# The tail of a decoder kernel's first step in two halves with a bank each, one VectorE division and one ScalarE copy moved forward near the end

## The chip, the cores and the metric

The kernel runs on one core of a Trainium2 chip. The metric is the device time of one execution in microseconds (us), taken as the median of several runs; smaller is better. One execution was also recorded by the hardware profiler, and all rows below come from that one. Times in rows are counted from the start of its span.

## What is computed

The reference is one decoder layer over 16 sequences of 128 tokens and 256 channels: a retention block, a cross-attention block and a feed-forward block, each behind a layer norm and added to its input. Cut to what matters:

```python
x = x + retention(layernorm(x))       # 8 heads of 32
x = x + attention(layernorm(x), ctx)  # 16 heads of 16, causal
x = x + ffn(layernorm(x))             # 8 experts, 256 -> 1024 -> 256, gelu

# retention, the part that the first edit touches
ret   = (ret - mean) * rsqrt(var + 1e-5)      # per token and head of 32
ret   = ret.reshape(B, S, 256) * gn_w + gn_b
gated = x @ W1
out   = (gated * sigmoid(gated) + ret) @ W2
# attention, the part that the second and third edit touch
attn = softmax(where(causal, -inf, q @ k.T * scale))
out  = (attn @ v) @ Wo + bo
```

Expert e serves sequences 2e and 2e + 1, so the kernel's unit of work, two sequences, needs one expert's weights.

## The kernel before, in words

The work is cut into 8 steps of 256 tokens (two sequences, `NB = 2`, of `P = 128` tokens). The three blocks form a software pipeline: iteration `i` of `body` works on the retention of step `a = i`, the attention of step `b = i - 1` and the feed-forward of step `c = i - 2`. Iterations 0, 1, 2 and 7, 8, 9 are written out (with the flags `do_a`, `do_b`, `do_c` and `nextA` saying which blocks take part), 3 to 6 are a hardware loop. Every engine has its own `body`; the order of instructions on an engine is the order of the code, written by hand, and the engines meet through counting semaphores (`signal`, `wait_ge`, `then_inc`). There is no scheduler. Only iteration 0 has a single block in it, so its engines have little else to do while a result goes from one to the next.

**Iteration 0, tail.** The retention output of both sequences lies in PSUM bank `a1` (two halves of 256 columns, one a sequence). GpSimd makes the 16 values of `rstA` (8 heads by 2 sequences) from `varA` with a power of minus one half (`rsqrt`, L454). VectorE multiplies the bank by them into `rnA`, which shares memory with `retT` and is called so in the rows (L1132). TensorE transposes the four 128x128 blocks into bank `a0` (L1671), VectorE scales them with `gn_sb` and adds the gate `silA` to give `outT` (L1151), TensorE multiplies by `W2_sb` into bank `a1` (`to_tokens`, semaphore `s_yA`), VectorE adds `x_keep` to give `x1` (L1161), takes the layer-norm statistics (`statB`, `mvB`), GpSimd makes `rsB`, VectorE normalises into `xnB` (L864), and TensorE transposes `xnB` at the start of iteration 1 (`query_input`, L1246). `projection_low(4, ...)` (the low part of Wo, `xWo_lo`) and the copy of the feed-forward bias (`b1T`) stand on VectorE between the multiplication and the gating. `keep_awake(n)` is `n` matmuls of zeros into a bank that nobody reads: they keep TensorE's activity up while it waits.

**Iteration 7** (`do_b and not nextA`). The softmax sums and the weighted values of a sequence arrive in bank `c0` by `values_to_tokens(seq)` on TensorE (L1422). `divide(seq)` on VectorE is a reciprocal of 16 columns (`rden`, L935) and a multiplication (`att`, L937). `values_to_tokens(1)` writes the same bank, so TensorE waits for `divide(0)` (`s_att`) before it. Behind `values_to_tokens(1)` TensorE has `keys(b0)` and `queries(a, a0)` of step 7, then the score matmuls of iteration 8. ScalarE takes the keys out of PSUM (`kB`, L625), then the queries (`qB`, L638).

**Iteration 8** (`not do_a`). ScalarE's row is: two of four roundings of the second feed-forward weight (`round_w2(2)`, `round_w2(3)`, in the rows `w_hi`), four exponentials (`exps(4)`), the copy of the transposed probabilities (`probT_even(2)`), `exps(5)`, and `ffn_input(b3)` (`xTC_hi`). The third and fourth pair of weight roundings are followed by GpSimd's subtraction (`w2_low`). TensorE's `prob_transposes(3)` needs the copy, because both use bank `b1k`.

## Time and profile before

| | |
|---|---|
| median of 3 runs | 350.05 us |
| the three runs | 350.05, 348.89, 350.06 us |
| the profiled execution | 348.83 us |
| its span, first to last instruction | 347.0 us |
| busy: TensorE, VectorE, ScalarE, GpSimd | 94%, 73%, 69%, 46% |
| granted TensorE clock, mean | 1.000 |

The profiled execution is near the fastest of the three runs, and 1.2 us below their median; 1.8 us of it lie outside the span. A busy share is a mean over the whole span: iterations 0, 1, 8 and 9 are less full than the loop, and there the engines wait for one another.

### The profile page before, as it was taken

To read this page: it belongs to the slowest core of one execution; us is meant where nothing else is said; L and a number is where in the kernel's file an instruction comes from. 1 tells how busy PE (TensorE), PEld (TensorE's weight loads), DVE (VectorE), ACT (ScalarE), POOL (GpSimd) and SP (SyncE) were. 2 spreads that over 40 slices of the span, in tenths; PEclk is the share of its full clock that TensorE was granted. 3 is DMA by queue.
4 is the path that set the end of the run, shared out by engine and by line. 5 is a ranking of instruction groups with operands and counts; after the bars stand their busy time and mean duration, and the time that the engine had idled before them with its cause. 6 is when DMAs were issued, how large, how long until landed. Compare 5 with 4: busy or idle time off the path is not lost.

```text
span 347.0 us, 9380 instructions
## 1 busy us (share of the span) xinstructions
PE 327.2 (94%) x3475; PEld 275.4 (79%) x3475; DVE 254.3 (73%) x559; ACT 238.7 (69%) x585; POOL 160.6 (46%) x144
## 2 busy tenths in 40 slices
PE   8788788999999999999999999999999998979796
PEld 3556556898889888898889888888889887858796
DVE  5664767687777886787777886797777877584884
ACT  4362556679858878679848877679848887797350
POOL 3645441190845458190846458190836362641100
PEclk9999999999999999999999999999999999999999
DMA  5990100404005400523005400423004300405000
GB/s 141 280 283 11 33 0 2 153 13 142 4 16 183 153 2 2 151 73 125 0 15 181 151 0 3 168 62 114 0 21 178 121 2 17 153 1 139 0 32 30
DMA packets 22458, 27.36 MB, mean 79 GB/s; under 512 B 2944, under 2 KB 20160, under 8 KB 22432
## 3 DMA queue, kind: packets, MB, share of 16 engines
q1 hardware_dynamic: 21616, 26.91, 24.8%
q8 instruction: 17, 0.28, 0.3%
q10 hardware_dynamic: 816, 0.10, 0.2%
q14 instruction: 9, 0.07, 0.1%
HBM read 24.51 MB, written 2.10 MB: 77 GB/s over the span
## 4 chain that ended last, share of the span: by engine, by line
PE 75%; issue 9%; DVE 7%; POOL 4%; ACT 3%; DMA 1%; DVEq 0%; ACTq 0%; POOLq 0%
PE c L1231 21%; PE a L1231 15%; PE b L1231 13%; PE b1k L1395 7%; PE b1k L1231 6%; PE b2k L1231 4%; PE c L1422 2%; PE a L1246 1%; POOL w_lo L467 1%; DVE scD L900 1%; DVE negmax L919 1%; PE b L1246 1%; PE b2k L1246 1%; PE b1k L1246 1%; PE c L1246 1%
## 5 line engine op out<-in xcount | busy, mean ns | idle before, releaser
L454 POOL TENSOR_TENSOR rstA<-varA,minus_half 128x16 f32<-128x16 f32 x8 | 23.4, 2928 | 62.5 <-DVE varA L1070 62.5
L603 ACT ACTIVATE prob<-b,negmax 128x128 f32<-128x128 f32 x124 | 35.8, 387 | 15.5 <-DVE negmax L919 15.5
L1395 PE MATMUL b1k<-ident,prob 128*128 128x128 f32 x256 | 39.7, 277 | 4.0 <-ACT probT L565 1.8
L467 POOL TENSOR_TENSOR w_lo<-w_in,w_hi 128x512 fp32r<-128x512 f32 x28 | 35.4, 1299 | 13.1 <-ACT w_hi L565 8.2
L565 ACT ACTIVATE w_hi<-w_in 128x512 fp32r<-128x512 f32 x64 | 37.8, 639 | 2.6 <-PE b L1231 2.6
L461 POOL TENSOR_TENSOR w_lo<-w_in,w_hi 128x512 fp32r<-128x512 f32 x28 | 35.0, 1282 | 7.3 <-ACT w_hi L565 5.6
L1395 PEld LDWEIGHTS b1k<-ident,prob 128*128 128x128 f32 x256 | 28.5, 141 | 9.6 <-ACT prob L603 3.9
L1231 PE MATMUL c<-xTC_hi,w_hi 128*128 128x256 f32 x108 | 31.9, 295 | 0.5
L919 DVE TENSOR_REDUCE negmax<-b 128x4 f32<-128x512 f32 x31 | 21.3, 687 | 13.3 <-PE a L1231 8.2
L454 POOL TENSOR_TENSOR rsC<-mvC,minus_half 128x2 f32<-128x2 f32 x8 | 5.7, 715 | 53.8 <-DVE mvC L856 53.8
L1231 PE MATMUL c<-xTC_lo,w_hi 128*128 128x256 f32 x108 | 30.5, 282 | 0.0
L1231 PE MATMUL c<-xTC_hi,w_lo 128*128 128x256 f32 x108 | 30.4, 282 | 0.0
L1231 PE MATMUL c<-w_hi,h_hi 128*128 128x256 f32 x96 | 30.0, 313 | 0.0
L926 DVE COPY probT<-b1k 128x512 f32<-128x512 f32 x32 | 22.0, 686 | 10.8 <-PE b1k L1395 10.8
L580 ACT ACTIVATE h_in<-c,b_cur 128x256 f32<-128x256 f32 x54 | 22.7, 472 | 10.3 <-PE c L1231 9.5
L1231 PE MATMUL c<-w_lo,h_hi 128*128 128x256 f32 x96 | 26.9, 280 | 0.0
L1231 PE MATMUL c<-w_hi,h_lo 128*128 128x256 f32 x96 | 26.9, 280 | 0.0
L912 DVE TENSOR_TENSOR h_lo<-h_in,h_hi 128x512 fp32r<-128x512 f32 x32 | 24.5, 765 | 1.1
L565 ACT ACTIVATE probT<-b1k 128x512 f32<-128x512 f32 x32 | 20.2, 631 | 5.7 <-PE b1k L1395 5.0
L1231 PEld LDWEIGHTS c<-xTC_hi,w_hi 128*128 128x128 f32 x108 | 20.6, 190 | 3.0 <-issue 2.2
L1231 PEld LDWEIGHTS c<-xTC_lo,w_hi 128*128 128x128 f32 x108 | 20.6, 191 | 0.0
L1231 PEld LDWEIGHTS c<-xTC_hi,w_lo 128*128 128x128 f32 x108 | 20.6, 191 | 0.0
(305 smaller groups left out, 1121.3 us busy)
## 6 DMA issues: line engine op xcount, KB each, us to landing
w_in<-in_L_ffn_w SPq DMA_DIRECT2D x16, 1024.0 KB, 5.6
x_in<-in_x SPq DMA_DIRECT2D x8, 256.0 KB, 2.8
c_in<-in_ctx SPq DMA_DIRECT2D x8, 256.0 KB, 3.2
out<-x2b SPq DMA_DIRECT2D x7, 256.0 KB, 2.2
b_cur<-in_L_ffn_b SPq DMA_DIRECT2D x8, 128.0 KB, 2.9
W_sb<-in_L_attn_W SPq DMA_DIRECT2D x2, 256.0 KB, 4.4
decay_sb<-in_decay SPq DMA_DIRECT2D x1, 512.0 KB, 3.8
mask_bf<-mask_bf SPq DMA_DIRECT2D x3, 128.0 KB, 8.2
```

Of the source, the lines that this page charges most:

```text
L454: pool.tensor_tensor(out, in_, minus_half[:, 0:n], ALU.pow).then_inc(s_out, 1)
L461: pool.tensor_tensor(w1_lo[:, :, part], w1_in[:, :, part], w1_hi[:, :, part].bitcast(F32), ALU.subtract).then_inc(s_w1lo, 1)
L467: pool.tensor_tensor(w2_lo[:, part, :], w2_in[:, part, :], w2_hi[:, part, :].bitcast(F32), ALU.subtract).then_inc(s_w2lo, 1)
L565: nc.scalar.activation(out, in_, ACT.Copy).then_inc(done, 1)
L580: ins = nc.scalar.activation(h_in[:, u, k, :], bank[:, k * T:(k + 1) * T], ACT.Gelu_apprx_tanh, bias=b1_cur[:, f:f + 1])
L603: ins = nc.scalar.activation(prob[:, u % PR, g, :], score_banks[u][:, g * P:(g + 1) * P], ACT.Exp, bias=negmax[:, u, g:g + 1], scale=-1.0)
L912: nc.vector.tensor_tensor(h_lo[:, part, :], h_in[:, u, :, :], h_hi[:, part, :].bitcast(F32), ALU.subtract).then_inc(s_hlo, 1)
L919: nc.vector.tensor_reduce(negmax[:, u, :], score_banks[u][:, :].rearrange("p (g m) -> p g m", g=G), AX_X, ALU.min).then_inc(s_max, 1)
L926: nc.vector.tensor_copy(probT[:, u % PR, :, :], b1k[:, :].rearrange("p (g n) -> p g n", g=G)).then_inc(s_pTd, 1)
L1231: return nc.tensor.matmul(out, lhsT, rhs, start=start, stop=stop)
L1246: ins = nc.tensor.transpose(out[:, col:col + P], src[:, b, k * P:(k + 1) * P], ident[:, :])
L1395: ins = nc.tensor.transpose(b1k[:, g * P:(g + 1) * P], prob[:, u % PR, g, :], ident[:, :])
```

## The change

Three edits. (1) In iteration 0 the normalisation, the transposes, the gating, the W2 product and the addition are done for one sequence after the other. The two sequences get banks of their own: `a0` and `b0` for the transposes, `b3` and `b2k` for the product. GpSimd's power becomes two of 8 values. VectorE's `projection_low(4, ...)` moves behind the statistics and `b1T` behind the gating. Three zero matmuls ahead of the W2 product are gone. (2) In iteration 7 `divide(0)` moves ahead of the addition that gives `x1`. (3) In iteration 8 `probT_even(2)` and `exps(4)` stand ahead of `round_w2(3)`.

```diff
@@ GpSimd
-                if do_a:
+                if isinstance(i, int) and i == 0:
+                    rsqrt(0, rstA[:, 0:RH], varA[:, 0:RH], s_varA, 2, s_rst_half, RH)
+                    rsqrt(0, rstA[:, RH:NB * RH], varA[:, RH:NB * RH], s_varA, 2, s_rstA, RH)
+                elif do_a:
                     rsqrt(a, rstA[:, :], varA[:, :], s_varA, 2, s_rstA, NB * RH)
@@ ScalarE, iteration 8
                     round_w2(2)
+                    probT_even(2)
+                    exps(4)
                     round_w2(3)
-                    exps(4)
-                    probT_even(2)
                     exps(5)
@@ VectorE
+                def first_normalised(bk, s_rst, s_done):
+                    heads = slice(RH * bk, RH * (bk + 1))
+                    dve.wait_ge(s_rst, 1)
+                    nc.vector.tensor_tensor(rnA[:, heads, :],
+                                            ret_bank[:, bk * D:(bk + 1) * D].rearrange("p (h e) -> p h e", e=RD),
+                                            rstA[:, heads].unsqueeze(2).broadcast_to([P, RH, RD]), ALU.mult)\
+                        .then_inc(s_done, 1)
+                def first_gated(bk, bank, s_in, s_done):
+                    tok = slice(bk * P, (bk + 1) * P)
+                    dve.wait_ge(s_in, 1)
+                    dve.wait_ge(s_sgA, 2)
+                    for k in range(C):
+                        nc.vector.scalar_tensor_tensor(out=outT[:, k, tok], in0=bank[:, k * P:(k + 1) * P],
+                                                       scalar=gn_sb[:, 0, k:k + 1], in1=silA[:, k, tok],
+                                                       op0=ALU.mult, op1=ALU.add).then_inc(s_done, 1)
+                if isinstance(i, int) and i == 0:
+                    first_normalised(0, s_rst_half, s_rn_half)
+                    first_normalised(1, s_rstA, s_rnA)
+                    first_gated(0, a0, s_rnT_half, s_outT_half)
+                    first_gated(1, b0, s_rnT, s_outT)
+                    dve.wait_ge(s_b1T, 1)
+                    nc.vector.tensor_copy(b1T[:, :], c0[:, 0:STEPS * FC]).then_inc(s_b1Tc, 1)
+                    dve.wait_ge(s_yA_half, 1)
+                    dve.wait_ge(s_keep, 1)
+                    nc.vector.tensor_tensor(x1[:, 0, :], b3[:, 0:D], x_keep[:, 0, :], ALU.add).then_inc(s_x1_half, 1)
+                    dve.wait_ge(s_x1_half, 1)
+                    nc.vector.bn_stats(statB[:, 0, :], x1[:, 0, :]).then_inc(s_lnB, 1)
+                    dve.wait_ge(s_yA, 1)
+                    nc.vector.tensor_tensor(x1[:, 1, :], b2k[:, 0:D], x_keep[:, 1, :], ALU.add).then_inc(s_x1, 1)
+                    dve.wait_ge(s_x1, 1)
+                    statistics(0, x1, statB, mvB, s_lnB, (1,))
+                    projection_low(4, 3, xWo_hi, xWo_lo)
+                    normalise(0, x1, mvB, rsB, xnB, s_rsB, s_xnB, s_TxB)
+                    return
...
-                if isinstance(i, int) and i == 0:
-                    projection_low(4, 3, xWo_hi, xWo_lo)
-                    dve.wait_ge(s_b1T, 1)
-                    nc.vector.tensor_copy(b1T[:, :], c0[:, 0:STEPS * FC]).then_inc(s_b1Tc, 1)
...
                 if do_b:
                     probT_odd(5)
+                if do_b and not nextA:
+                    divide(0)
                 if do_a:
                     dve.wait_ge(s_yA, a + 1)
...
                     split_transposed(s_cTB, a, b0, cTB_hi, cTB_lo, s_cTBlo)
-                    divide(0)
                     add_ffn(c)
                     divide(1)
@@ TensorE
-                if do_a:
+                if isinstance(i, int) and i == 0:
+                    for bk, (bank, s_in, s_done) in enumerate(((a0, s_rn_half, s_rnT_half), (b0, s_rnA, s_rnT))):
+                        pe.wait_ge(s_in, 1)
+                        for k in range(C):
+                            src = rnA[:, RH * bk:RH * (bk + 1), :].rearrange("p h e -> p (h e)")
+                            ins = nc.tensor.transpose(bank[:, k * P:(k + 1) * P], src[:, k * P:(k + 1) * P], ident[:, :])
+                        ins.then_inc(s_done, 1)
+                elif do_a:
                     pe.wait_ge(s_rnA, a + 1)
...
-                if do_a:
-                    if isinstance(i, int) and i == 0:
-                        keep_awake(3)
+                if isinstance(i, int) and i == 0:
+                    pe.wait_ge(s_W2, 16)
+                    for bk, (bank, s_in, s_done) in enumerate(((b3, s_outT_half, s_yA_half), (b2k, s_outT, s_yA))):
+                        pe.wait_ge(s_in, C)
+                        for k in range(C):
+                            ins = mm(bank[:, 0:D], outT[:, k, bk * P:(bk + 1) * P], W2_sb[:, k, :],
+                                     start=(k == 0), stop=(k == C - 1))
+                        ins.then_inc(s_done, 1)
+                elif do_a:
                     pe.wait_ge(s_outT, 2 * (a + 1))
-                    if isinstance(i, int) and i == 0:
-                        pe.wait_ge(s_W2, 16)
                     to_tokens(a1, (outT,), (W2_sb,), s_yA)
```

This is VectorE's order in the tail of iteration 0 in the kernel before, from the multiplication by `rstA` to `xnB`.

```order
L1132 TENSOR_TENSOR retT<-a,rstA 128x512
L1061 SCALAR_TENSOR_TENSOR xWo_lo<-h_in,xWo_hi 128x512
L1138 COPY b1T<-c 128x64
L1151 SCALAR_TENSOR_TENSOR outT<-a,gn_sb,silA 128x256 x2
L1161 TENSOR_TENSOR x<-a,x_keep 128x512
L849 BN_STATS statB<-x 128x6 x2
L853 BN_AGGR mvB<-statB 128x2 x2
L856 TENSOR_SCALAR mvB<-mvB 128x2
L864 TENSOR_SCALAR xnB<-x,mvB,rsB 128x256 x2
```

This is the same place on VectorE in the changed kernel (its lines are numbered anew).

```order
L1141 TENSOR_TENSOR retT<-a,rstA 128x256 x2
L1152 SCALAR_TENSOR_TENSOR outT<-a,gn_sb,silA 128x128 x2
L1152 SCALAR_TENSOR_TENSOR outT<-b,gn_sb,silA 128x128 x2
L1162 COPY b1T<-c 128x64
L1165 TENSOR_TENSOR x<-b,x_keep 128x256
L1167 BN_STATS statB<-x 128x6
L1169 TENSOR_TENSOR x<-b2k,x_keep 128x256
L858 BN_STATS statB<-x 128x6
L862 BN_AGGR mvB<-statB 128x2 x2
L865 TENSOR_SCALAR mvB<-mvB 128x2
L1070 SCALAR_TENSOR_TENSOR xWo_lo<-h_in,xWo_hi 128x512
L873 TENSOR_SCALAR xnB<-x,mvB,rsB 128x256 x2
```

Every 512-column operation is now two of 256 and every 256-column gating two of 128; the low part of Wo went from ahead of the gating to behind the statistics, and the first sequence's statistics stand ahead of the second's addition.

This is VectorE's order in iteration 7 of the changed kernel, from the gating to the low part of the normalised queries' input.

```order
L1194 SCALAR_TENSOR_TENSOR outT<-a,gn_sb,silA 128x256 x2
L935 COPY probT<-b1k 128x512
L944 RECIPROCAL rden<-c 128x16
L946 TENSOR_TENSOR att<-c,rden 128x256
L1206 TENSOR_TENSOR x<-a,x_keep 128x512
L858 BN_STATS statB<-x 128x6 x2
...
L878 TENSOR_TENSOR cTB_lo<-b,cTB_hi 128x512
L996 TENSOR_TENSOR x2b<-c,x2b 128x512
L944 RECIPROCAL rden<-c 128x16
L946 TENSOR_TENSOR att<-c,rden 128x256
L878 TENSOR_TENSOR xTB_lo<-a,xTB_hi 128x512
```

The upper pair `rden`, `att` (the division of the first sequence) stood between `cTB_lo` and `x2b` before; the lower pair has not moved.

## Rows read from the trace of the kernel before

**Rows 1.** The page: TensorE's busy time, and the granted clock in 40 slices.
```profile
PE 327.2 (94%) x3475; PEld 275.4 (79%) x3475; DVE 254.3 (73%) x559; ACT 238.7 (69%) x585; POOL 160.6 (46%) x144
...
PEclk9999999999999999999999999999999999999999
```

**Rows 2.** Chain that ended last, in order of time (start us, us, what).
```profile
19.52 2.91 POOL rstA L454
22.43 6.97 issue
```

**Rows 3.** Timeline of VectorE, iteration 0 (start us, us, operation, [idle before]).
```profile
22.46 0.69 DVE L1132 TENSOR_TENSOR retT<-a,rstA 128x512 f32<-128x512 f32 x1 [0.58 <-POOL rstA L454]
...
23.91 0.88 DVE L1151 SCALAR_TENSOR_TENSOR outT<-a,gn_sb,silA 128x256 f32<-128x256 f32 x2
26.87 0.69 DVE L1161 TENSOR_TENSOR x<-a,x_keep 128x512 f32<-128x512 f32 x1 [2.09 <-PE a L1231]
27.59 0.75 DVE L849 BATCH_NORM_STATS2 statB<-x 128x6 f32<-128x256 f32 x2
...
30.17 0.74 DVE L864 TENSOR_SCALAR xnB<-x,mvB,rsB 128x256 f32<-128x256 f32 x2 [0.81 <-POOL rsB L454]
```

**Rows 4.** Timeline of TensorE, iteration 0.
```profile
21.91 1.04 PE L1231 MATMUL c<-awake 128*128 128x512 bf16 x4
23.21 0.66 PE L1671 MATMUL a<-ident,retT 128*128 128x128 f32 x4 [0.27 <-DVE retT L1132]
...
24.83 1.99 PE L1231 MATMUL a<-W_sb,outT 128*128 128x256 f32 x8 [0.32 <-DVE outT L1151]
...
29.35 1.03 PE L1231 MATMUL c<-awake 128*128 128x512 bf16 x4
30.96 0.66 PE L1246 MATMUL b<-ident,xnB 128*128 128x128 f32 x4 [0.58 <-DVE xnB L864]
```

**Rows 5.** Groups by line and shape (xcount | busy us, mean ns | idle before us).
```profile
L454 POOL TENSOR_TENSOR rstA<-varA,minus_half 128x16 f32<-128x16 f32 x8 | 23.4, 2928 | 62.5 <-DVE varA L1070 62.5
L454 POOL TENSOR_TENSOR rsB<-mvB,minus_half 128x2 f32<-128x2 f32 x8 | 5.7, 707 | 22.9 <-DVE mvB L856 22.9
...
L1151 DVE SCALAR_TENSOR_TENSOR outT<-a,gn_sb,silA 128x256 f32<-128x256 f32 x16 | 7.0, 478 | 0.2 <-PE a L1671 0.2
...
L937 DVE TENSOR_TENSOR att<-c,rden 128x256 f32<-128x256 f32 x14 | 5.9, 425 | 0.5
```

**Rows 6.** Timeline of VectorE, iteration 7.
```profile
289.36 0.69 DVE L1161 TENSOR_TENSOR x<-a,x_keep 128x512 f32<-128x512 f32 x1 [1.84 <-PE a L1231]
...
293.53 0.25 DVE L935 RECIPROCAL rden<-c 128x16 f32<-128x16 f32 x1
...
295.68 0.68 DVE L869 TENSOR_TENSOR xTB_lo<-a,xTB_hi 128x512 fp32r<-128x512 f32 x1
```

**Rows 7.** Timelines of TensorE and of ScalarE, iteration 7.
```profile
286.99 0.60 PE L1422 MATMUL c<-ident,pvT 128*128 128x128 f32 x4
...
294.38 0.63 PE L1422 MATMUL c<-ident,pvT 128*128 128x128 f32 x4 [0.66 <-DVE att L937]
...
292.72 0.60 ACT L565 ACTIVATE pvT<-b 128x512 f32<-128x512 f32 x1
...
296.45 1.93 ACT L625 ACTIVATE kB<-b,bk_of,head_of 128x256 f32<-128x256 f32 x4 [2.09 <-PE b L1231]
```

**Rows 8.** Timelines of ScalarE and of TensorE, iteration 8.
```profile
306.33 1.21 ACT L565 ACTIVATE w_hi<-w_in 128x512 fp32r<-128x512 f32 x2
...
310.30 0.60 ACT L565 ACTIVATE xTC_hi<-b 128x512 fp32r<-128x512 f32 x1 [0.21 <-PE b L1246]
...
306.59 0.63 PE L1395 MATMUL b1k<-ident,prob 128*128 128x128 f32 x4
...
309.20 0.63 PE L1395 MATMUL b1k<-ident,prob 128*128 128x128 f32 x4 [1.41 <-ACT probT L565]
...
311.68 0.39 PE L1231 MATMUL a<-xTC_hi,w_hi 128*128 128x256 f32 x1
```

More of the change, by code:

```diff
@@ L296, in decoder_kernel @@
         s_yB_half = signal("s_yB_half")
+        s_rst_half = signal("s_rst_half")
+        s_rn_half = signal("s_rn_half")
+        s_rnT_half = signal("s_rnT_half")
+        s_outT_half = signal("s_outT_half")
+        s_yA_half = signal("s_yA_half")
+        s_x1_half = signal("s_x1_half")
         s_x2_half = signal("s_x2_half")
```

## The prediction

> **What bounds the kernel now.** The page comes first. TensorE is busy 94% of the span and its granted clock is at the upper level, 2.4 GHz, in all 40 slices [rows 1]. So the loop in the middle is TensorE's, and nothing here touches the loop. A gain can come only from stretches in which TensorE waits, and every wait that is shortened there moves all that follows. Next I read the chain that ended last, at the places of the edits. At the tail of iteration 0 it goes through GpSimd's power, and then shows 6.97 us as "issue" [rows 2]: there nothing is full, a result is handed from engine to engine. The timelines show these hands [rows 3, 4]: multiply (from 22.46), transpose (23.21), gate (23.91), W2 product (24.83), addition (26.87), statistics (27.59), `xnB` (30.17), and TensorE goes on at 30.96. In this stretch TensorE's real work is 0.66 and 1.99 us, and VectorE sits idle 2.09 us ahead of the addition. From `xnB` on iteration 1 depends on it throughout: scores, maxima and retention of step 1 all come behind its queries. In iteration 7 TensorE stands still 0.66 us for `att` [rows 7], although the sums for it were in the bank at 287.59. In iteration 8 TensorE waits 1.41 us for the copy of the probabilities [rows 8].
>
> **Edit 1, the halves.** I follow both sequences by the clock of the profile.
>
> GpSimd: 16 values cost 2.93 us, 2 cost 0.71 [rows 5]. A straight line through the two gives 0.158 us for a value and 0.39 us fixed, so 8 values cost 1.66. The first half is ready at 19.52 + 1.66 = 21.18, the second at 22.84, 0.41 later than the whole was [rows 2]. The bounds are 0.71 and 2.93 for one half.
>
> VectorE: 256 columns cost 0.42 us [rows 5] against 0.69 for 512 [rows 3]. The second multiplication runs 22.88 to 23.30. TensorE is at its four zero matmuls until about 22.8 (a new one every 0.21) [rows 4], so the first two transposes run 22.8 to 23.2 (four cost 0.66, each further one 0.12, two about 0.42) and the second two 23.36 to 23.78. Gating 256 columns costs 0.48 [rows 5], and the second begins 0.40 after the first, since the two take 0.88 [rows 3]; by the slope above 128 columns cost 0.35, with a start every 0.27, so a pair costs 0.62. First sequence: 23.30 to 23.92. Second: 23.84 to 24.46. TensorE starts the W2 product of the first at 23.96; eight records last 1.99 [rows 4], the second sequence follows without a gap, and all is done at 25.95 instead of 26.82. Here the split has taken the late start of GpSimd's second half and the extra fixed times and still gained 0.87.
>
> Behind it the split pays again. The first sequence's addition and statistics (from 25.0 to 25.9) lie beside the second product. After 25.95 there is one addition of 256 columns (0.42 instead of 0.69) and one statistic (0.43; both were 0.75), with a handover of 0.03 or 0.04 each: end of the statistics at 25.99 + 0.42 + 0.03 + 0.43 = 26.87 instead of 28.34 [rows 3]. That is **1.47 us**, and the rest, GpSimd's `rsB` and `xnB`, follows as before.
>
> What hides the rest: the low part of Wo (0.68, 0.60 to the next start) now stands between the last `mvB` operation and `xnB`. VectorE waits 0.81 there for GpSimd [rows 3], so it fits with 0.2 to spare; without that cover it would cost its 0.6. `b1T` lies in the wait for the product. The three zero matmuls gone cost nothing and give nothing, since TensorE waited behind them in any case. On TensorE the transposes of `xnA`, the gate matmuls and the last four zero matmuls move by 0.87 only. These ended at 30.38 [rows 4] and so will end at 29.51, with the last one issued about 0.17 before that; `xnB` will be there at 30.91 - 1.47 = 29.44. The two meet: I count 1.45. Bounds: 0.87 if the zero matmuls and the handovers eat the rest, 1.9 if GpSimd's half costs nearer 1.4 and the gating of 128 columns nearer 0.25.
>
> A rule speaks against such halves. The row is that 512 columns take 0.69 us and 256 take 0.42 [rows 3, 5], so each cut costs a fixed 0.15. The Trainium skill ("VectorE: DVE Perf Modes", section on the TRN2 errata) says that each VectorE instruction pays a fixed latency, and advises tiles of 512 elements or more. Its formula for PSUM input would give 258 ns for a gating of 128 columns, so an estimate by that page has the pair at 0.52 instead of 0.62 and edit 1 gains 0.1 more. The trace agrees that there is a fixed part; here it falls on an engine that waits.
>
> **Edit 2, the division.** It needs `values_to_tokens(0)`, which ends at 287.59 [rows 7]. VectorE is then in the 1.84 us that it waits for the W2 product ahead of 289.36 [rows 6]. The pair runs 287.63 to 288.34, 1.0 us before the addition can start: hidden. If `values_to_tokens(0)` came more than 1.0 later, it would delay `x1` by the excess. Taken out at 293.53, it leaves TensorE free to start `values_to_tokens(1)` right behind the transposes of `xnB`, about 293.53, with its input `pvT` there at 293.32 [rows 7]. Before it started at 294.38: 0.85 us. `keys` follow at once; their input `cTB_lo` ends where the division used to start, about 293.6, ahead of the new start at 293.9. VectorE's second division and `xTB_lo` (295.68) [rows 6] move by 0.9, so the queries don't wait longer either. ScalarE takes `kB` when the keys are done (it idles 2.09 before) [rows 7], and its queries and iteration 8's scores hang on that. The step from the last operation's end to the new start is 0.02 shorter or longer; I count **0.83**. Bounds: 0 if something else holds the keys, 0.9.
>
> **Edit 3, the copy.** TensorE's transposes that the copy reads end at 306.59 + 0.63 = 307.22 [rows 8]. The first rounding frees ScalarE at about 306.9, so ScalarE now waits some 0.35 for them. Then everything is the same work, and `xTC_hi` stands at its end in both orders. Before, ScalarE had a wait of 0.21 to 0.39 ahead of `xTC_hi` (310.30, the lower figure by ends, the upper by the next possible start) and this is used up. TensorE's wait of 1.41 shrinks by more than a microsecond, but the work behind it then meets the next wait, at 311.68, for the split of `xTC`, which follows `xTC_hi`. So I count **0.03 lost**, with bounds of 0.2 lost and 0.27 gained (how soon TensorE could have been at 311.68 if the split were there).
>
> **The sum.** 1.45 + 0.83 - 0.03 = 2.25 us, from the profiled execution's 348.83 to 346.6 (span 344.75). The median of the runs shown is 1.2 above that execution. The three runs lie in two groups, near 348.9 and near 350.05; I take their mean, 349.67, as the start and name 347.4.
>
> **The rivals.**
> - *GpSimd's power does not scale*: with 2.93 for each half the second multiplication starts at 25.4, the product of the second sequence ends about 28.1, the statistics at 29.0, 0.7 later than now. With edit 2 the whole gains 0.1: 349.5. For it: only two sizes are known. Against it: these two differ by four times. Chance 0.05.
> - *The lead of iteration 0 is used up in iterations 1 and 2* (a load, or the zero matmuls there): only edit 2 is left, 0.8, 348.8. For it: iteration 1 has its own waits. Against it: they hang on the same chain, and the power of iteration 1 starts only when its own variance is there. Chance 0.13.
> - *Edit 2 gives nothing* because ScalarE or VectorE is late for another reason: 1.4, 348.2. Chance 0.14.
> - *Slower: the clock*. Three zero matmuls are gone between 23.7 and 24.8, where TensorE did least. If the granted clock fell from 2.4 to 1.2 GHz there, the product would take 4.0 instead of 2.0, the transposes, gate matmuls and zero matmuls behind it another 3 more, and TensorE would reach `xnB`'s transposes about 4 us later than now: with edit 2, 352.9. Each us of TensorE's work at the lower level costs one more, so it decides from 2.3 us of such work. Against it: TensorE idles only 0.1 to 0.2 there after the change, less than the 0.27, 0.32 and 0.58 that stand in this stretch now at full clock [rows 4]. The Trainium skill ("TensorE: Matmul & The Clock Gate", section on the HAM clock gate) says that a TensorE that has idled is put back to half its clock. By that rule the removal costs nothing either unless the idle time is long. Chance 0.04; other losses 0.03.
>
> **How the numbers follow.** The forecast has 0.55, more than it (2.9, from the upper bounds) 0.06. The range goes from the gain of 2.9 on the fast runs, 346.0, to edit 2 alone on the runs' upper group, 349.2. A measurement of this kernel tells about 0.5% from no change, 1.75 us. The forecast passes it by 0.5, and with the spread of its terms lands below it once in ten; edit 1 alone passes it rarely. Faster 0.68, same 0.27, slower 0.05.
>
> **What would show it.** In the trace after: two powers of about 1.7 us; the second half of the W2 product ending near 25.9; `xnB` at 28.7 instead of 30.17 and TensorE's transposes of it near 29.5; full clock throughout; in iteration 7 `values_to_tokens(1)` without a wait and the gap from `xnB`'s transposes to the scores of iteration 8 shorter by 0.8; in iteration 8 the wait ahead of `xTC`'s product as long as TensorE's wait for the copy has become shorter. The prediction is wrong if the distance from `xnB` of iteration 0 to the loop grows by what was gained, or if the power of 8 costs over 2.2.

## The result and the profile after

The changed kernel takes 347.04 us (median of 8 runs, 346.94 to 348.35); the kernel before, run beside it, 349.96 us (8 runs, 348.80 to 350.08). The ratio is 0.9943 [0.9928, 0.9958]: 0.57% faster, about 2.0 us, just past the 0.5% that a measurement of this kernel can tell from no change; the interval's near end, 0.42%, lies inside it. The forecast was 347.4 in 346.0 to 349.2.

The runs of either kernel fall in two groups by the granted clock that each run records. With a mean of 1.000 the changed kernel takes 346.94 to 347.09 (5 runs), with 0.995 it takes 348.34 or 348.35 (3 runs). Of the kernel before, two runs lie near 348.85 and six near 350.0. Group against group the gain is 1.9 and 1.7 us; the first stands on only two runs of the kernel before. The plain medians differ by 2.9, because more runs of before fell in the upper group. In what follows "at full clock" means the runs at 1.000 or 0.999, and the numbers of different kernels are compared within that group.

The profiled execution of the changed kernel is one of the upper group: its own time is 348.34, its span 346.5, against 348.83 and 347.0 before. So the end of this trace holds something that the trace of before doesn't, and I read the places of the edits first. The page, TensorE's busy time and the granted clock in 40 slices; beside [rows 1] one slice near the end is no longer full:

```profile
PE 327.9 (95%) x3472; PEld 277.0 (80%) x3472; DVE 254.8 (74%) x563; ACT 238.7 (69%) x585; POOL 161.8 (47%) x145
...
PEclk9999999999999999999999999999999999999989
```

GpSimd after, iteration 0, its timeline (start us, us, operation, [idle before]):

```profile
19.49 3.86 POOL L460 TENSOR_TENSOR rstA<-varA,minus_half 128x8 f32<-128x8 f32 x2 [0.80 <-DVE varA L1079]
28.04 1.07 POOL L460 TENSOR_TENSOR rsB<-mvB,minus_half 128x2 f32<-128x2 f32 x1 [4.70 <-DVE mvB L865]
```

The view of the tile `rstA` after, from 19 to 24 us, gives the two halves apart (count, least, median and greatest duration in ns, first and last start):

```profile
L460 POOL TENSOR_TENSOR rstA<-varA,minus_half x2: 1806/2026/2246, 19.5 to 21.1; 128x8 f32<-128x8 f32 x2
```

The first half is recorded with 1.81 us, the second with 2.25, and the two overlap by 0.2. Together they take 3.86 where 3.32 were forecast. On VectorE the first gating stands behind the second multiplication, so everything from the first gating on waits for the second half; only the first sequence's transposes, from 22.75, make use of the first. And `rsB`, 0.71 before and in every other iteration [rows 5], takes 1.07. VectorE after, iteration 0, its timeline:

```profile
21.17 0.69 DVE L1070 SCALAR_TENSOR_TENSOR xWq_lo<-h_in,xWq_hi 128x512 fp32r<-128x512 f32 x1
21.77 0.42 DVE L1141 TENSOR_TENSOR retT<-a,rstA 128x256 f32<-128x256 f32 x1
23.38 0.42 DVE L1141 TENSOR_TENSOR retT<-a,rstA 128x256 f32<-128x256 f32 x1 [1.20 <-POOL rstA L460]
23.72 0.60 DVE L1152 SCALAR_TENSOR_TENSOR outT<-a,gn_sb,silA 128x128 f32<-128x128 f32 x2
...
26.93 0.43 DVE L858 BATCH_NORM_STATS2 statB<-x 128x6 f32<-128x256 f32 x1
27.51 0.25 DVE L862 BATCH_NORM_AGGREGATE mvB<-statB 128x2 f32<-128x6 f32 x2 [0.16 <-DVE statB L858]
...
27.87 0.68 DVE L1070 SCALAR_TENSOR_TENSOR xWo_lo<-h_in,xWo_hi 128x512 fp32r<-128x512 f32 x1
29.15 0.74 DVE L873 TENSOR_SCALAR xnB<-x,mvB,rsB 128x256 f32<-128x256 f32 x2 [0.59 <-POOL rsB L460]
```

The second multiplication starts at 23.38 (22.88 forecast), the statistics end at 27.36 (26.87), and `xnB` starts at 29.15 (28.70) where it was 30.17 [rows 3]. TensorE after, in iteration 0 and then in iteration 7, its timelines:

```profile
24.47 1.10 PE L1275 MATMUL b<-W_sb,outT 128*128 128x256 f32 x4 [0.17 <-DVE outT L1152]
25.41 1.03 PE L1275 MATMUL b2k<-W_sb,outT 128*128 128x256 f32 x4
...
28.96 1.03 PE L1275 MATMUL c<-awake 128*128 128x512 bf16 x4
29.94 0.66 PE L1290 MATMUL b<-ident,xnB 128*128 128x128 f32 x4
...
292.18 0.66 PE L1290 MATMUL a<-ident,xnB 128*128 128x128 f32 x4 [0.42 <-DVE xnB L873]
292.67 0.60 PE L1466 MATMUL c<-ident,pvT 128*128 128x128 f32 x4
```

The transposes of `xnB` start at 29.94 instead of 30.96 [rows 4]: edit 1 gives 1.02 us there, not 1.45. In iteration 7 the transposes of `pvT` follow without a wait, where 0.66 stood [rows 7]. The first scores of iteration 8 come at 297.43 (299.16 before), of which 0.89 was there at 292.18 already (293.07 before), so edit 2 gives 0.84. In iteration 8 TensorE's wait for the copy is 0.20 instead of 1.41 [rows 8]; TensorE then waits 0.20 for VectorE's copy of other probabilities (at 308.20), and after it for the product of `xTC`:

```profile
309.97 0.39 PE L1275 MATMUL a<-xTC_hi,w_hi 128*128 128x256 f32 x1 [0.76 <-DVE xTC_lo L878]
```

It stood at 311.68 [rows 8], 1.71 later; the lead was 1.73 at the scores, so edit 3 costs 0.02. At this point the trace has 1.71 us of gain. At its end only 0.52 are left: the last `x1b` starts at 343.59, before at 344.11. The windows of the end of this trace (columns: the stretch, busy time of each engine, the granted clock, DMA):

```profile
core 0: us, PE busy (x) PEld busy (x) DVE busy (x) ACT busy (x) POOL busy (x), PEclk, DMA share, GB/s
325.00:327.00 2.00, 0.19 (x2) 0.00 (x0) 1.93 (x8) 0.00 (x0) 0.81 (x1) 1.00 0.00 0
327.00:328.00 1.00, 0.87 (x6) 0.87 (x7) 0.96 (x4) 0.17 (x1) 0.85 (x1) 0.82 0.00 0
328.00:331.00 3.00, 3.00 (x16) 3.00 (x15) 2.97 (x4) 0.43 (x1) 0.62 (x1) 0.50 0.02 5
331.00:332.00 1.00, 1.00 (x10) 1.00 (x10) 0.00 (x0) 0.00 (x0) 0.00 (x0) 0.97 0.00 0
```

From 325.2 to 327.1 TensorE does nothing (it waits 1.94 us for `xnC` of the last step). Then the granted clock is 0.50 of 2.4 GHz, that is 1.2 GHz, for some 3 us, and 16 matmuls pass in 3 us. In the kernel before's trace, behind a wait of 1.95 that ends at 328.85, 25 pass in the matching 3 us (329.8 to 332.8) at 1.00.

### The profile page after: what moved, and what is told of

Same layout as the page of the kernel before. It is cut to its first block, busy times and chain, and to the rows that moved or that the text cites. A ratio compares the mean times of both kernels' runs of the same rounds, so it can differ in the third digit from the quotient of the medians.

```text
span 346.5 us, 9380 instructions
## 1 busy us (share of the span) xinstructions
PE 327.9 (95%) x3472; PEld 277.0 (80%) x3472; DVE 254.8 (74%) x563; ACT 238.7 (69%) x585; POOL 161.8 (47%) x145
## 2 busy tenths in 40 slices
DMA packets 22458, 27.36 MB, mean 79 GB/s; under 512 B 2944, under 2 KB 20160, under 8 KB 22432
## 4 chain that ended last, share of the span: by engine, by line
PE 76%; issue 7%; DVE 7%; POOL 4%; ACT 3%; DMA 1%; ACTq 0%; DVEq 0%; POOLq 0%
PE c L1275 22%; PE a L1275 15%; PE b L1275 14%; PE b1k L1439 7%; PE b1k L1275 6%; PE b2k L1275 4%; PE a L1290 2%; PE c L1466 2%; POOL w_lo L473 1%; DVE scD L909 1%; DVE negmax L928 1%; POOL rstA L460 1%; DMA wk_c<-in_L_attn_Wk 1%; PE b2k L1290 1%; PE b1k L1290 1%
## 5 line engine op out<-in xcount | busy, mean ns | idle before, releaser
L460 POOL TENSOR_TENSOR rstA<-varA,minus_half 128x16 f32<-128x16 f32 (+1 forms) x9 | 24.4, 2730 | 62.5 <-DVE varA L1079 62.5
```

Source lines behind the costliest of these rows:

```text
L460: pool.tensor_tensor(out, in_, minus_half[:, 0:n], ALU.pow).then_inc(s_out, 1)
```

## The experiments

Each line "at full clock" below is a median of those runs, with the kernel before on the same chip in brackets. No experiment changes what is computed; zero matmuls write a bank that nobody reads. The experiments ran on three chips, and the kernel before differs between them by up to 0.3 us at full clock (348.64 to 348.92), so gains are compared rather than times.

**Edit 1 alone.** The changed kernel with the division and the copy put back:

```diff
-                if do_b and not nextA:
-                    divide(0)
...
                     split_transposed(s_cTB, a, b0, cTB_hi, cTB_lo, s_cTBlo)
+                    divide(0)
                     add_ffn(c)
...
-                    probT_even(2)
-                    exps(4)
                     round_w2(3)
+                    exps(4)
+                    probT_even(2)
```

> Edit 1 alone. If the halves are worth what the trace of the change shows at TensorE's transposes of xnB (30.96 before, 29.94 after, so 1.02 us) and the loop keeps it, like runs are 0.9 to 1.0 us faster than before, and the transposes of xnB stand near 29.94 again. The rival that the gain at the start is used up in iterations 1 and 2 has like runs within 0.2 us of before. The two powers of 8 values take 1.8 and 2.2 us again.

Measured: 347.9, ratio 0.9986 [0.9969, 1.0003]; at full clock 347.82 (348.64), 0.82 less. The interval over all runs includes no change; at full clock the two kernels' runs don't overlap (347.48 to 347.92 against 348.42 to 348.86). In its trace the transposes of `xnB` start at 29.96, `rsB` takes 1.07, and iteration 7 is reached at 292.16, 0.91 ahead of before. So of some 1.0 us at the start 0.8 to 0.9 comes out (0.9 to 1.0 was expected), and the size is short of 1.45 at the start itself, not lost on the way.

**Edit 2 alone.**

```diff
+                if do_b and not nextA:
+                    divide(0)
...
                     split_transposed(s_cTB, a, b0, cTB_hi, cTB_lo, s_cTBlo)
-                    divide(0)
                     add_ffn(c)
```

> Edit 2 alone. If the division moved forward is worth the 0.85 us that it takes out of TensorE's row in iteration 7, like runs are 0.8 us faster than before and the wait of 0.66 us ahead of the second transposes of pvT is gone. The rival that it needs the lead of edit 1, or that the keys are held by something else, has less than 0.3 us.

Measured: 347.97, ratio 0.9976 [0.9961, 0.9991]; at full clock 347.88 (348.64), 0.77 less. From the transposes of `xnB` (293.32) to the first scores (298.57) it is 5.25 us, as in the changed kernel (292.18 to 297.43), and 6.09 in before: 0.84.

**Edit 3 alone.**

```diff
                     round_w2(2)
+                    probT_even(2)
+                    exps(4)
                     round_w2(3)
-                    exps(4)
-                    probT_even(2)
```

> Edit 3 alone. The prediction has 0.03 us lost, with ScalarE waiting 0.2 to 0.4 us for TensorE and TensorE's wait of 1.41 us going over into one ahead of the product with xTC_hi. So like runs are within 0.1 us of before. The rival that the copy helps TensorE on the path gives 0.3 us or more.

Measured: 348.79, ratio 1.0001 [0.9987, 1.0016]; at full clock 348.73 (348.64), 0.09 more, which is inside the scatter of the runs. Its trace shows the wait move: 0.20 instead of 1.41 for the copy, and 0.75 for `xTC_lo` at 311.74.

Singly the three edits give 0.82, 0.77 and -0.09, together 1.50, where the changed kernel gives 1.9 by its runs and 1.71 by its trace. The single edits were run on another chip, and the 1.9 has two runs of before under it, so the 0.2 to 0.4 between them isn't settled.

**The power of 8 where VectorE is quiet.** Why was the second half 0.6 too long? The kernel before, with the power of iteration 7 cut in two, where both halves are awaited together:

```diff
-                if do_a:
+                if do_a and not nextA:
+                    rsqrt(a, rstA[:, 0:RH], varA[:, 0:RH], s_varA, 2, s_rst_half, RH)
+                    rsqrt(a, rstA[:, RH:NB * RH], varA[:, RH:NB * RH], s_varA, 2, s_rstA, RH)
+                elif do_a:
                     rsqrt(a, rstA[:, :], varA[:, :], s_varA, 2, s_rstA, NB * RH)
```

> The kernel before, with GpSimd's power of 16 values in two of 8 in iteration 7, where VectorE is idle for 1.5 us of it. If the 1.81 and 2.25 us of the halves in iteration 0 come from VectorE's work beside them, the two take about 1.66 each here, 3.3 together. If a power of 8 values costs more than the line through 2 and 16 gives, for reasons of its own, they take 1.8 to 2.2 each here too, 3.7 or more together. The end of the run is not what this one is for: at most 0.4 us slower.

Measured: 348.59 in one run. GpSimd's timeline in its trace, iteration 7:

```profile
280.59 3.27 POOL L455 TENSOR_TENSOR rstA<-varA,minus_half 128x8 f32<-128x8 f32 x2 [8.55 <-DVE varA L1074]
```

By the tile's view these are 1.64 and 1.66 us: the straight line through 16 and 2 values was right (1.66). VectorE does nothing from 280.5 to 282.0 there, and from 282.0 on, beside the second half, it reduces a PSUM bank; neither half is longer for that. So the length of 2.25 in iteration 0 belongs to the place.

**The low part of Wq moved behind the first multiplication.** In the changed kernel the second power starts at about 21.10, and `xWq_lo` runs from 21.17. It reads two operands from SBUF, and GpSimd reads its operand there too.

```diff
-                    projection_low(3, 0, xWq_hi, xWq_lo)
...
                     first_normalised(0, s_rst_half, s_rn_half)
+                    projection_low(3, 0, xWq_hi, xWq_lo)
                     first_normalised(1, s_rstA, s_rnA)
```

> The changed kernel with the low part of Wq moved from ahead of the first multiplication to behind it. Theory of the blocked read: at the second power's start (21.1) VectorE now works on the first multiplication, which reads one operand of 256 columns from PSUM, so the second power costs about 1.7 instead of 2.25 and ends near 22.9. The second transposes come about 0.5 earlier; like runs are 0.3 to 0.5 us faster than the changed kernel. The rival leaves it at 2.25 and the time where it is.

Measured: 346.51, ratio 0.9925 [0.9903, 0.9947]; at full clock 346.45 (348.92), 2.48 less. GpSimd, then VectorE, in its trace:

```profile
19.37 3.25 POOL L460 TENSOR_TENSOR rstA<-varA,minus_half 128x8 f32<-128x8 f32 x2 [0.80 <-DVE varA L1079]
27.36 1.07 POOL L460 TENSOR_TENSOR rsB<-mvB,minus_half 128x2 f32<-128x2 f32 x1 [4.74 <-DVE mvB L865]
...
21.54 0.68 DVE L1070 SCALAR_TENSOR_TENSOR xWq_lo<-h_in,xWq_hi 128x512 fp32r<-128x512 f32 x1
22.66 0.42 DVE L1140 TENSOR_TENSOR retT<-a,rstA 128x256 f32<-128x256 f32 x1 [0.43 <-POOL rstA L460]
```

The pair takes 3.25 instead of 3.86, and everything up to the transposes of `xnB` comes 0.56 earlier against the power's start (table below); 0.3 to 0.5 was expected of the runs, and they give 0.6. By the tile's view the halves are 1.80 and 1.65. The first is still 0.15 longer than in the quiet place, but that lies in its overlap with the second: the pair takes what it took there, 3.27. `xWq_lo` now starts while GpSimd is at work on the second half, and neither is longer for it.

**The low part of Wo ahead of the first multiplication.** This tests both at once: behind `xWq_lo` stands a second such operation, and none is left beside `rsB`.

```diff
+                    projection_low(4, 3, xWo_hi, xWo_lo)
                     first_normalised(0, s_rst_half, s_rn_half)
...
-                    projection_low(4, 3, xWo_hi, xWo_lo)
                     normalise(0, x1, mvB, rsB, xnB, s_rsB, s_xnB, s_TxB)
```

> The changed kernel with the low part of Wo ahead of the first multiplication instead of beside GpSimd's rsB. Theory: a VectorE operation with two SBUF inputs keeps GpSimd from reading its own input, so GpSimd's small power waits for its end. Then rsB falls from 1.07 to 0.71 us, and the second power of 8 values grows from 2.25 to about 2.85, since xWo_lo follows xWq_lo at once. The rival (the two powers in a row are slow for reasons of their own) leaves the second at 2.25. In time: 0.4 gained at rsB, up to 0.6 lost at the second half, 0.2 lost on the whole or nothing.

Measured: 348.6, ratio 0.997 [0.9956, 0.9985]; at full clock 347.55 (348.92), 1.38 less. GpSimd, then TensorE, in its trace:

```profile
19.61 4.46 POOL L460 TENSOR_TENSOR rstA<-varA,minus_half 128x8 f32<-128x8 f32 x2 [0.80 <-DVE varA L1079]
28.77 0.70 POOL L460 TENSOR_TENSOR rsB<-mvB,minus_half 128x2 f32<-128x2 f32 x1 [4.70 <-DVE mvB L865]
...
29.89 0.81 PE L1275 MATMUL c<-awake 128*128 128x512 bf16 x3
30.54 0.60 PE L1290 MATMUL b<-ident,xnB 128*128 128x128 f32 x4
```

The pair is longer by one more operation of VectorE's (4.46 less 3.86 is 0.60, VectorE's distance from one such operation to the next), and `rsB` is back at 0.70. GpSimd's length follows what VectorE reads when GpSimd starts. In time this order is 0.5 worse than the changed kernel, by the runs (1.38 less than before, not 1.9) and by the trace (the transposes 10.93 behind the power's start, not 10.45), where 0.2 or nothing was expected. `xnB` is 0.23 later, the 0.60 lost less the 0.37 regained; the other 0.25 are the zero matmuls ahead of iteration 1, which were left out of the expectation and stand in TensorE's row until 30.54, while `xnB`, begun at 29.50, is done at 30.23.

**The whole power, halves behind it.** The changed kernel with the one power of 16 values of before:

```diff
-                    rsqrt(0, rstA[:, 0:RH], varA[:, 0:RH], s_varA, 2, s_rst_half, RH)
-                    rsqrt(0, rstA[:, RH:NB * RH], varA[:, RH:NB * RH], s_varA, 2, s_rstA, RH)
+                    rsqrt(0, rstA[:, :], varA[:, :], s_varA, 2, s_rstA, NB * RH)
...
-                    first_normalised(0, s_rst_half, s_rn_half)
+                    first_normalised(0, s_rstA, s_rn_half)
```

> The changed kernel with one power of 16 values again, the halves starting behind it. The power ends at 22.40, so the first multiplication starts at 22.44 (21.77 in the changed kernel) and the second at about 22.80 (23.38). TensorE's second transposes come at about 23.3 instead of 23.86 and the W2 product ends near 25.9 instead of 26.44. The zero matmuls and xnB follow 0.5 earlier, so like runs are about 0.5 us faster than the changed kernel. If the late second half does not matter, because something else holds the second sequence, nothing changes.

Measured: 347.31, ratio 0.9935 [0.9913, 0.9958]; at full clock 346.76 (348.92), 2.16 less, 0.2 to 0.3 better than the changed kernel's 1.9. The power takes 2.90 and everything behind it is halved: cutting GpSimd's power cost more than it gave, as it was placed. The expectation was 0.5 better; in the trace it is 0.33, since the first gating now waits for the first sequence's transposes:

```profile
23.22 0.61 DVE L1151 SCALAR_TENSOR_TENSOR outT<-a,gn_sb,silA 128x128 f32<-128x128 f32 x2 [0.20 <-PE a L1713]
```

An order in which the first gating stands ahead of the second multiplication, and so could use an early first half, wasn't tried.

**Zero matmuls in the wait of iteration 9.** The other difference in the trace is the clock at the end. The changed kernel, and then the kernel before, with eight zero matmuls ahead of the transposes of `xnC`, once the work of the step before is out:

```diff
                     down_of_both(c - 1, 1)
+                    pe.wait_ge(s_hT, UP * (c - 1) + 3)
+                    keep_awake(8)
                     ffn_input(a0)
```

> The changed kernel with eight zero matmuls in TensorE's wait of 1.94 us ahead of the transposes of xnC in iteration 9. Theory: the two groups of times (346.95 and 348.34 in the runs of the changed kernel) differ by a fall of the granted clock to 1.2 GHz behind this wait. Then the zero matmuls keep the clock, all runs lie in the lower group at clock 1.000, and the median falls to that group's. The rival (the fall comes from elsewhere) leaves both groups. Eight at 0.21 take 1.7 us, so they fit in the wait.

> The kernel before with the eight zero matmuls in iteration 9 alone. If the fall of the clock behind that wait makes the two groups of the kernel before as well, all runs are at clock 1.000 and lie near 348.8, the median 0 to 1.2 us under that of before by how many of its runs fell. The rival leaves both groups.

Measured: the changed kernel with them 347.08 (346.77 to 347.21), ratio 0.9929 [0.9911, 0.9948]; all 6 runs at full clock. The kernel before with them 348.85 (348.59 to 349.06), ratio 0.9983 [0.9969, 0.9997]; all 12 at full clock, beside 14 of 23 runs of before on the same chip in the upper group, at 350.03. TensorE's timeline in the trace of the first, and its windows at the end:

```profile
325.13 1.67 PE L1275 MATMUL c<-awake 128*128 128x512 bf16 x7
327.00 0.66 PE L1290 MATMUL a<-ident,xnC 128*128 128x128 f32 x4 [0.20 <-DVE xnC L873]
```

```profile
328.00:331.00 3.00, 2.96 (x25) 2.75 (x24) 3.00 (x5) 0.40 (x2) 0.51 (x1) 1.00 0.00 0
```

Where 16 matmuls passed at 0.50, 25 pass at 1.00. So the upper group of the kernel before and of the changed kernel is this fall of the clock; the upper runs of the other versions have the same mean clock, 0.99 to 0.995. The zero matmuls themselves cost little: 0.1 to 0.2 us by the runs at full clock (348.85 against 348.67 on one chip; the changed kernel gains 1.84 over before with them and 1.9 without, on different chips).

**No zero matmuls in iteration 0 of before.** The forecast looked for a fall of the clock here, since edit 1 drops three of them.

```diff
-                    if isinstance(i, int) and i == 0:
-                        keep_awake(3)
```

> The kernel before without the three zero matmuls ahead of the W2 product of iteration 0. The prediction's slower rival was that their removal lets the clock fall there. If so, the granted clock from 24 to 30 us is below 1.00 in some runs, the product's 1.99 us grow, and the mean of the runs is up to some us slower. If not, the clock stays at 1.00 there and like runs are within 0.15 us of before.

Measured: 348.98, ratio 0.9997 [0.998, 1.0013]; at full clock 348.85 (348.67). They do nothing at this place that these runs can show (0.18 between like medians, expected within 0.15), and the clock stays at 1.00 there.

**All together.** The changed kernel with `xWq_lo` behind the first multiplication, `xWo_lo` between the second gating and `b1T` (in VectorE's wait for the product, with no GpSimd work beside it), and the eight zero matmuls of iteration 9; the second of the two kernels also has two zero matmuls instead of four ahead of iteration 1:

```diff
                     first_gated(1, b0, s_rnT, s_outT)
+                    projection_low(4, 3, xWo_hi, xWo_lo)
...
                 if nextA and not do_b:
-                    keep_awake(4)
+                    keep_awake(2)
```

> The same with all four zero matmuls ahead of iteration 1. Theory: in the changed kernel these end when xnB is ready, so an earlier xnB (rsB at 0.71 instead of 1.07) is of no use as long as they stand: 0.3 us slower than with two, and equal within 0.1 to the kernel with xWq_lo alone at full clock (346.44). The rival that TensorE waits for xnB alone makes it as fast as with two.

> All that the runs point to, on the changed kernel: xWq_lo behind the first multiplication, xWo_lo between the second gating and the copy b1T, where GpSimd has nothing to read, two instead of four zero matmuls ahead of iteration 1, and eight in the wait of iteration 9. The powers of 8 take 1.8 and 1.65 us, rsB 0.71, xnB comes 0.37 earlier than in the kernel with xWq_lo alone, and TensorE can take it then. At full clock 346.1, and no run in the lower level, so a median 2.9 us or more under that of before. If the two zero matmuls fewer let the clock fall, TensorE's matmuls of iteration 1 get longer and the time is above 347.

Measured: 346.31 (346.05 to 346.42), ratio 0.9907 [0.9884, 0.993], with four zero matmuls, and 346.14 (345.77 to 346.28), ratio 0.9904 [0.988, 0.9927], with two; all 12 runs at full clock. Both beat the kernel before; against their own chip's 348.67 at full clock they gain 2.36 and 2.53, the changed kernel 1.9. `xWq_lo` moved alone gains 2.48, so what they add at full clock, less the cost of the eight zero matmuls, is within the scatter; what they add for certain is that no run falls to the upper group. Two zero matmuls instead of four are worth 0.17 by the runs, 0.27 in the traces, and 0.3 was expected; the rival that TensorE waits for `xnB` alone falls. GpSimd, VectorE and TensorE in the trace of the last (span 344.3):

```profile
19.63 3.25 POOL L460 TENSOR_TENSOR rstA<-varA,minus_half 128x8 f32<-128x8 f32 x2 [0.80 <-DVE varA L1079]
27.63 0.69 POOL L460 TENSOR_TENSOR rsB<-mvB,minus_half 128x2 f32<-128x2 f32 x1 [4.75 <-DVE mvB L865]
...
24.39 0.68 DVE L1070 SCALAR_TENSOR_TENSOR xWo_lo<-h_in,xWo_hi 128x512 fp32r<-128x512 f32 x1
28.36 0.74 DVE L873 TENSOR_SCALAR xnB<-x,mvB,rsB 128x256 f32<-128x256 f32 x2 [0.81 <-POOL rsB L460]
...
28.54 0.59 PE L1275 MATMUL c<-awake 128*128 128x512 bf16 x2
29.15 0.66 PE L1290 MATMUL b<-ident,xnB 128*128 128x128 f32 x4
```

The traces don't all start iteration 0's tail at the same instant, so the kernels are compared by the distance from the start of the first power to the start of `xnB` and of TensorE's transposes of it:

| kernel | power | `rsB` | to `xnB` | to its transposes |
|---|---|---|---|---|
| before | 2.91 | 0.70 | 10.65 | 11.44 |
| changed | 3.86 | 1.07 | 9.66 | 10.45 |
| whole power | 2.90 | 1.07 | 9.33 | 10.12 |
| Wo early | 4.46 | 0.70 | 9.89 | 10.93 |
| Wq late | 3.25 | 1.07 | 9.10 | 9.89 |
| all, four zero matmuls | 3.25 | 0.70 | 8.74 | 9.79 |
| all, two zero matmuls | 3.25 | 0.69 | 8.73 | 9.52 |

## Why the prediction was right

The range, the sign and the likeliest case held. One term of the sum was wrong in size, and that the median came within 0.4 of the forecast has luck in it (below, on the clock).

**Edit 1, 1.45 forecast, 1.02 in the trace.** Down to `xnB` 1.47 was forecast and 1.02 came. Three parts make up the difference. *The second half of the power* was to be ready at 22.84 and was at 23.35; the product ended at 26.44 instead of 25.95: 0.49 less gain. The first half's 21.18 gave the forecast nothing, since the order of VectorE ties the rest to the second. The length of 1.66 was right, as the quiet power shows. What failed was that it was taken as free of what stands beside it. The prediction's own sign of being wrong was a power of 8 over 2.2, and the second half came at 2.25: the term failed by that sign, though the sum stayed in its range. *The low part of Wo* "fits with 0.2 to spare": on VectorE it did, but it made `rsB` 0.36 longer, and GpSimd is on the path there: 0.36 less gain. *A stall of VectorE went away*: in before its two `mvB` aggregations start 0.47 apart,

```profile
28.50 0.18 DVE L853 BATCH_NORM_AGGREGATE mvB<-statB 128x2 f32<-128x6 f32 x1 [0.16 <-DVE statB L849]
28.97 0.18 DVE L853 BATCH_NORM_AGGREGATE mvB<-statB 128x2 f32<-128x6 f32 x1 [0.29 <-issue]
```

and after they follow in 0.07 (27.51, two in 0.25): 0.40 more gain, which I hadn't seen, since I carried over the stretch from the statistics to `rsB` "as before". 1.47 less 0.49 less 0.36 plus 0.40 is 1.02. The stall stands in all six traces with before's order of the tail and in none of those with the halves. What it waits for, the profile doesn't show, and I didn't try to find it; without this 0.40, which I hadn't forecast, the term would have come to an estimated 0.62 (1.02 less 0.40), under its lower bound of 0.87, which was given for other reasons.

**The zero matmuls and `xnB` meet**, as said: in the changed kernel's trace they are done issuing at 29.8 and `xnB` at 29.89, so they don't bind yet. In the version with all moves and four of them they do, by 0.27 (9.79 against 9.52 in the table).

**Edit 2, 0.83 forecast, 0.84 in the trace, 0.77 by the runs of it alone.** All steps as told: the addition of `x1` still waits for its product (1.01 instead of 1.84), the keys follow at once.

**Edit 3, 0.03 lost forecast, 0.02 in the trace.** The wait of 1.41 became 0.20. The forecast wanted the 1.21 back ahead of the product of `xTC`; 0.76 stand there, 0.20 ahead of it for `probT`, and about 0.3 ahead of the transposes of `xnC`, which start 0.76 behind the ones before them where it was 0.46.

**The lead in the loop.** 1.02 at iteration 0 is 0.89 at iteration 7, so 0.13 is lost; where isn't settled. The rival that took it all falls.

**The clock.** "Full clock throughout" was wrong. The clock rival named the right mechanism at the wrong place: in the tail of iteration 0 TensorE's waits are at most 0.73 us, and even the kernel before without its three zero matmuls, where one is 0.97, stays at full clock there. So does every trace behind the wait of 1.71 us at about 14.8. The wait after which it does fall is 1.95 us long in iteration 9 and stood in the trace of before, at full clock in that execution. The two groups of runs, which I took as unexplained and bridged by a mean, are executions with and without this fall. With the mean as the start the forecast of 347.4 was 0.4 above the result: at full clock the sum of 2.25 would have given 346.6 and the runs gave 346.96. And the measured median lies in the lower group because five of eight runs did; with the majority the other way, as in the kernel before, it would have been 348.3, in the range but 0.9 above the forecast.

## What to carry to other kernels

In this kernel a short GpSimd operation on the path cost what it costs alone only where VectorE wasn't reading two operands from SBUF when it started: look at what stands beside its start, not at its whole length, before cutting it in two or putting "free" work into its shadow. And cut a step in two only where the order behind it lets the first half be used. When runs of one kernel fall in two groups, ask the granted clock of each run first, then look for TensorE's longest wait in a profile of the slower group; eight zero matmuls there cost 0.1 to 0.2 us and took 1.1 to 1.4 off about half of the runs here.

## What the runs showed of the hardware

**GpSimd waits for VectorE at its start.** Taking the quiet length off each end, the second power could begin its work at 23.35 less 1.65, 21.70, while `xWq_lo` was recorded until 21.86; with two such operations in a row at 24.07 less 1.65, 22.42, the second one recorded until 22.57; `rsB` at 29.11 less 0.70, 28.41, with `xWo_lo` until 28.55. Each time it is 0.14 to 0.16 ahead of the recorded end of VectorE's operation. GpSimd's own recorded start says little here: the second power is recorded from 21.10, ahead of `xWq_lo` at 21.17, and waits for it all the same. That GpSimd is held is shown by the moves in both directions; that it is held until just this point is worked out from three places. Operations of VectorE with one operand in PSUM don't do it: in before the power of iteration 0 starts beside `cTB_lo` (19.35 to 20.04) and takes 2.91, as in the other iterations.

The Trainium skill ("SBUF — State Buffer", section "SBUF: two separate sides") says that VectorE with two SBUF inputs and a GpSimd operation that reads SBUF share a pair of ports as an exclusive lock, and that the other one is fully blocked. These traces agree: 0.6 us for one such operation, 1.2 for two, nothing for none. The same place says that whoever starts first holds the ports for its whole instruction. No trace here shows that of GpSimd: with the power of 16 values under way from 19.52 to 22.43 in before, the low parts of Wv and Wq (19.95 and 21.20) take their usual 0.68, and in the version with Wq late `xWq_lo` starts at 21.54, in the middle of the second half, and takes 0.68. The measurement decides: here GpSimd's small power kept VectorE from nothing once it was going. Which part of it reads SBUF wasn't tried.

**The clock after a wait.** Behind the same wait of 1.94 to 1.95 us of TensorE two traces (the changed kernel and the whole power) have some 3 us at 1.2 GHz, and eight have none. Nothing is seen in any trace behind the next longest, 1.71 us. The runs record only a mean clock: 14 of 23 executions of the kernel before on one chip, 8 of 17 and 11 of 29 on two others, have the 0.994 or 0.995 that goes with such a stretch, the others 1.000. Eight zero matmuls in that wait (325.1 to 326.8 in the trace shown) kept it at 2.4 GHz (a mean of 0.999 or 1.000) in all 30 runs of the four kernels that had them.

**VectorE on 128 columns.** A pair of gatings of 128 columns takes 0.60 to 0.61 us, where the slope of the rows gave 0.62. The estimate by the Trainium skill ("VectorE: DVE Perf Modes", section on the TRN2 errata) was 0.52, so the rows decide.
